# Windowed attention with value regions gathered through DRAM, one Trainium2 core: the stores of the turned values move from SyncE's queue to GpSimd's

## The reference, cut to what matters

```python
qkv = jnp.einsum('nchw,oc->nohw', xc, qkv_w) + qkv_b[None, :, None, None]
q, k, v = jnp.split(qkv, 3, axis=1)
...
a_r = q_r @ k_r
_, idx_r = jax.lax.top_k(a_r, TOPK)
...
attn = jnp.einsum('bhnqd,bhnkd->bhnqk', qs * SCALE, key_g)
attn = jax.nn.softmax(attn, axis=-1)
out = jnp.einsum('bhnqk,bhnkd->bhnqd', attn, val_g)
...
out = out + lepe
out = jnp.einsum('nchw,oc->nohw', out, out_w) + out_b[None, :, None, None]
```

## Time and profile before

| | |
|---|---|
| median of 3 runs (lowest to highest) | 1795.88 us (1792.58 to 1802.46) |
| the profiled execution, its span | 1792.81 us, 1789.8 us |
| PE, DVE, ACT, POOL busy | 91%, 86%, 77%, 59% of the span |
| granted TensorE clock | 0.996 |
| queue of SP's DMAs, of POOL's DMAs | 24.7%, 16.7% of 16 DMA engines' time |

### The profile page before, as it was taken

One profiled execution on the slowest core, in us unless ns is written; L12 is line 12 of the kernel. 1 busy time (PEld: TensorE's weight loads), 2 busy tenths in 40 slices (PEclk: granted clock), 3 DMA queues, 4 the chain that ended last, 5 costly groups with the idle time before them and its releaser, 6 DMA issues.

```text
span 1789.8 us, 73643 instructions
## 1 busy us (share of the span) xinstructions
PE 1636.2 (91%) x26568; PEld 1377.4 (77%) x26568; DVE 1530.6 (86%) x2951; ACT 1383.9 (77%) x4401; POOL 1052.2 (59%) x2548
## 2 busy tenths in 40 slices
PE   5999999999999899899999999899899999999897
PEld 4877777887778777777777788788787878777676
DVE  6589888899889889888888889899898888889895
ACT  2488778888778788788888788788787888877674
POOL 3256556566566565655565566556556666577664
PEclk9999999999999999999999999999999999999998
DMA  5233434343434343344444444434343334366555
GB/s 200 77 97 120 126 103 139 108 149 117 127 113 137 107 149 115 116 123 122 126 119 129 123 126 121 125 107 151 105 127 102 115 103 129 113 203 196 196 185 191
DMA packets 164632, 234.43 MB, mean 131 GB/s; under 512 B 19232, under 2 KB 146912, under 8 KB 164272
## 3 DMA queue, kind: packets, MB, share of 16 engines
q1 hardware_dynamic: 141408, 129.71, 24.7%
q0 software_dynamic: 22864, 100.02, 16.7%
HBM read 166.80 MB, written 62.85 MB: 128 GB/s over the span
## 4 chain that ended last, share of the span: by engine, by line
PE 61%; DVE 11%; issue 10%; ACT 9%; POOL 4%; DMA 2%; SPq 2%; POOLq 1%; ACTq 0%; DVEq 0%
PE chunk_bank L1124 20%; PE pt_bank L1240 10%; PE s_bank L1218 10%; ACT probs L744 7%; PE o_bank L1258 6%; DVE neg_max L959 5%; PE o_bank L1240 4%; PE chunk_bank L1138 3%; DVE lepe L846 2%; PE o_bank L1266 2%; POOL k_sel L502 2%; PE chunk_bank L1166 2%; PE chunk_bank L1151 1%; POOL lepe L514 1%; DMA v_sel<-v_dram 1%
## 5 line engine op out<-in xcount | busy, mean ns | idle before, releaser
L744 ACT ACTIVATE probs<-s_bank,neg_max 128x256 f32<-128x256 f32 x1568 | 734.0, 483 | 240.7 <-DVE neg_max L959 240.7
L502 POOL COPY k_sel<-k_all 128x128 f32 x1568 | 397.1, 302 | 512.4 <-PE s_bank L1218 421.9
L959 DVE TENSOR_REDUCE neg_max<-s_bank 128x2 f32<-128x512 f32 x784 | 486.8, 682 | 161.2 <-PE s_bank L1218 160.6
L846 DVE SCALAR_TENSOR_TENSOR lepe<-v_band,taps,lepe 128x448 f32<-128x448 f32 x896 | 621.3, 743 | 0.0
L1124 PE MATMUL chunk_bank<-xn,wqkv 128*128 128x224 f32 x2544 | 588.9, 357 | 29.0 <-ACT v_stage L711 13.4
L1124 PEld LDWEIGHTS chunk_bank<-xn,wqkv 128*128 128x128 f32 x2544 | 439.7, 192 | 40.9 <-issue 37.2
L754 ACT COPY probs_t<-pt_bank 128x512 f32<-128x512 f32 x611 | 364.5, 597 | 81.8 <-PE pt_bank L1240 79.3
L1240 PE MATMUL pt_bank<-ident,probs 128*128 128x128 f32 x2444 | 375.9, 276 | 22.4 <-ACT probs L744 13.3
L1240 PEld LDWEIGHTS pt_bank<-ident,probs 128*128 128x128 f32 x2444 | 281.4, 141 | 98.7 <-issue 69.4
L514 POOL TENSOR_TENSOR lepe<-o_norm,lepe 128x128 f32<-128x128 f32 x392 | 263.8, 692 | 150.7 <-DVE o_norm L982 147.3
L744 ACT ACTIVATION_READ_ACCUMULATOR probs<-s_bank,neg_max 128x1 f32 x1568 | 332.1, 212 | 0.0
(11 more groups left out here) (81 smaller groups left out, 1442.6 us busy)
## 6 DMA issues: line engine op xcount, KB each, us to landing
v_sel<-v_dram SPq DMA_DIRECT2D x1568, 64.0 KB
xn<-x_dram POOLq DMA_DIRECT2D x56, 448.0 KB, 4.9
v_dram<-v_stage SPq DMA_DIRECT2D x112, 224.0 KB
resid<-x_dram POOLq DMA_DIRECT2D x31, 448.0 KB, 4.6
out_dram<-resid POOLq DMA_DIRECT2D x31, 448.0 KB, 5.6
spill<-lepe POOLq DMA_DIRECT2D x25, 448.0 KB, 3.6
xn<-spill POOLq DMA_DIRECT2D x25, 448.0 KB, 5.5
resid<-x_dram POOLq DMA_DIRECT2D x25, 224.0 KB, 3.3
```

The source lines that it names most:

```text
L502: last = pool.tensor_copy(k_sel[:, r % K_SLOTS, :, RT * j:RT * (j + 1)], k_all[:, b % 2, :, bass.ds(reg[j] * RT, RT)])
L744: act.activation(probs[:, 2 * (j % 2) + i, :], s_bank[:, u, KEYS * at:KEYS * (at + 1)], ACT.Exp, bias=neg_max[:, h % 2, col:col + 1], accu ...
L846: ins = dve.scalar_tensor_tensor(row, v_band[:, n % BANDS, k, t // 3:t // 3 + RS, t % 3:t % 3 + W], taps[:, k, t:t + 1], row, ALU.mult, AL ...
L959: dve.tensor_reduce(neg_max[:, h % 2, 2 * j:2 * j + 2], scored, AX.X, ALU.max, negate=True).then_inc(max_done, 1)
```

## The change

Rows of image 0 are still stored by SP in the prologue. From row 7 on, `store_values` is a function of POOL's program, with the same two DMAs and two semaphores of its own, `v_kept`. POOL calls it at place 1 of the next step (`rc == 1 and rr`), so row 0's to row 5's stores stand one step later than their row; for an image's last row it calls it at place 5 of the row's own step, behind `normalize` and `load_resid`. SP's three calls are gone. The waits for stored rows, in `select_values` on SP and in `vt_out` on ACT, go through `wait_values`, which picks the semaphore by the row's number.

```diff
+        def wait_values(eng, n):
+            if n < NWIN:
+                eng.wait_ge(v_stored[n % 2], 32 * (n // 2 + 1))
+            else:
+                eng.wait_ge(v_kept[n % 2], 32 * ((n - NWIN) // 2 + 1))
...
                 if r % NREG == 0:
                     n = b * NWIN + LAST
-                    sp.wait_ge(v_stored[0], 32 * (n // 2 + 1))
-                    sp.wait_ge(v_stored[1], 32 * ((n + 1) // 2))
+                    wait_values(sp, n - 1)
+                    wait_values(sp, n)
...
                     r = s * NWIN + rc
-                    if rc == 4 and rr == LAST and is_row(kv):
-                        store_values(kv)
                     if is_region(r + 2):
                         select_values(r + 2)
-                    if rc == 0 and rr == 1 and is_row(kv - 1):
-                        store_values(kv - 1)
                     if rc == 1 and rr == LAST and is_row(kv):
                         load_index(kv // NWIN)
-                    if rc == 6 and rr not in (0, LAST) and is_row(kv):
-                        store_values(kv)
...
+            def store_values(n):
+                b, rr = divmod(n, NWIN)
+                for m in range(2):
+                    wait_taken(pool, "vt", n, m)
+                if b >= 2 and rr == 0:
+                    pool.wait_ge(attn_done, NREG * (b - 1))
+                for h in range(2):
+                    pool.dma_start(v_dram[b % 2, h:RS:2, rr * W:(rr + 1) * W, :].rearrange("q t d -> t q d"),
+                                   v_stage[PADW * h:PADW * h + W, n % 2, :, :]).then_inc(v_kept[n % 2], 16)
...
+                    if rc == 1 and rr and is_row(kv - 1):
+                        store_values(kv - 1)
+                    elif rc == 5 and rr == LAST and is_row(kv):
+                        store_values(kv)
...
                 if n >= 2:
-                    act.wait_ge(v_stored[n % 2], 32 * (n // 2))
+                    wait_values(act, n - 2)
```

More of the change, by code:

```diff
@@ L305, in attention_kernel @@
         v_stored = [sem(f"v_stored{i}") for i in range(2)]
+        v_kept = [sem(f"v_kept{i}") for i in range(2)]
         v_sel_in = [sem(f"v_sel_in{i}") for i in range(V_SLOTS)]
```

## The result

The changed kernel takes 1851.2 us (median of 4 runs, 1845.7 to 1854.0), against 1799.0 us for the kernel before, run beside it. The ratio is 1.0295, with a 95% interval from 1.0265 to 1.0326: slower by 52 us.

The account below looks back on a forecast made before the run. The prediction took PE, busy 91% of the span, as what bounds the kernel. Six image ends 27.6, image 6 7 and the clock 8.5 made 43 us, added to the profiled 1792.8: 1836 us, range 1815 to 1860.

Parts of the forecast that it names:

- the landing of the fourth load: SP's fourth value load for region 49 at an image end: estimated to land 2.5 us after issue.
- the clock: Half clock on PE behind waits of 5 us: 1.7 us at five of seven ends, 8.5 us (bounds 0 and 11.9).
- Off SP: Taking 49 rows' stores off SP's queue: worth at most 5.9 us to PE, taken as nothing.
- The 42 ordinary rows: Two issues on POOL at place 1, 1.3 us a row, covered by its waits for PE: costed at nothing.
- POOL's waits for scores: Sign in the profile after: POOL's waits for scores shorter by about 1.3 us in ordinary rows.
- Six image ends: Images 0 to 5: values land 9.05 us after `load_resid`, PE wants them at 3.8; net 4.6 us each, 27.6 us.
- The next duo's loads: Eight SP loads behind region 49's: land by about 16.1 us, PE wants them at 17.2, so the delay doesn't grow.
- What comes back: At each of six image ends, 0.65 us that PE waits for ACT shortly after is regained from the 5.25 us wait.
- Image 6: Last late end, where attention's first body is a duo: 7 us (bounds 2 and 11).
- the one with smaller waits: Rival at image ends: time given back or fast landings, 1815 us, or 1804 if half comes back too; chance 0.10.
- The one in which the store stays hidden: Rival at region 49's `attend`: values arrive in time, not slower, 1793 or 1787 us; chance 0.04.
- POOL as the bound: Rival in ordinary rows: each store issue keeps POOL 1.5 us, 47 us more, 1883 us; chance 0.06.

Follow-up runs that it names:

- experiment 1: The change, but the seven image-end stores are back on SP at their old place; 42 rows stay on POOL: 1792.2 us, 1.0007 of the kernel before.
- experiment 3: The change, but POOL issues the image-end store at place 3 instead of 5, all 49 rows on POOL: 1791.4 us, 0.9998 of the kernel before.
- Experiment 7: The change, with the x load moved from place 0 to place 3 in an image's first step: 1840.1 us, again 1840.4 against the change's 1848.1.
- experiment 6: The change plus needless matmuls ahead of the first region's `attend` of images 1 to 7: 1845.5 us with 24, 1835.2 with 12 (change beside it 1848.1).
- The kernel of place 4: The change, but POOL issues the image-end store at place 4, ahead of normalize, instead of 5: 1814.0 us, 1.0148 of the kernel before.
- the second run of the change: The change itself, unchanged, run again on a third chip beside its variants: 1848.1 us, 1.0325 of the kernel before.

## Why the prediction came out as it did

The direction and the mechanism were right, and 1851.2 us lies in the range; the predicted 1836 was 15 us short. The sizes of two terms were not right, the landing of the fourth load and the clock. Step by step:

- **Off SP: nothing.** Right. Experiments 1 and 3 equal the kernel before, and in 3 all 49 rows are off SP.
- **The 42 ordinary rows: nothing.** Right, by experiment 1. A pair of issues keeps POOL 1.38 us at the image end and 1.42 us in the row shown, against 1.3. But I had expected POOL's waits for scores to be shorter by about 1.3 us a row, some 55 us; they fell by 421.9 - 402.4 = 19.5 us. I had overlooked POOL's other pause, at `take_region`: by experiment 1 it took up 24.8 us and the waits for scores 35.0. In the change the waits at the late ends, where POOL stands for PE, add to both.
- **Six image ends, 9.05 us behind `load_resid`.** It is 11.5 us at image 0. Three terms held: the second issue at 0.69 (0.65), the landing 3.57 to 3.93 (3.6), SP's way to the fourth load 2.54 (2.3). The fourth failed: "the fourth lands 2.5 us later, an estimate between the 1.8 us [...] and the 8.48 us". It is 2.5 only where nothing follows (2.59 at image 5); five times it is 4.33 to 5.41, because POOL issues the x load of 448 KB at the same moment (305.92 and 305.93). So the six waits are 42.7 us, where 5.25 us each made 31.5. Experiment 7 shows the cause, and that it is worth about 8 us of time. Two smaller errors offset each other in the waits: the steps between the terms take some 0.6 us more, and PE comes some 0.8 us later. For the latter, POOL's next key copies do not lie under PE's wait, as I wrote, but hold up the scores ahead of it (301.83 above).
- **The next duo's loads: the delay doesn't grow.** Right: of the seven places only the last has a second wait (2.52 us).
- **What comes back, 0.65 us at each.** Right, but for one end. The first body of images 2 to 6 took 8.69, 8.62, 10.31, 8.69 and 8.62 us before, and takes 8.03 or 8.04 us behind a wait at full clock (experiment 6): 0.6 to 0.7 us come back at four ends, 2.3 us at the end of image 3.
- **Image 6: 7 us.** 5.7 us by its rows.
- **The clock: 8.5 us.** The mechanism was right, and experiment 6 shows it; the size was some 17 us: 17.5 by halving the slow work, or, at the six ends, 13.2 us by comparing the bodies with 8.03 us, where halving gives 14.0. I took the 3.5 us stretch of the earlier trace rows for the length of every one and left two ends out. All seven waits brought the clock down, and it stayed down for 3.1 to 5.8 us of work, 7.1 at image 6.

The seven places cost 63.9 us where my sum had 43; the two misjudged terms, 11 us of landings and some 8 to 9 us of clock, are most of the difference. The rest of the execution is 6.1 us shorter, which no term of mine foresaw, and so 15 us remain between the 1836 us and the profiled 1850.6. That the miss is no larger is in that part luck.

Of the rivals, the one with smaller waits fell because the waits were longer, not shorter, and little of them came back. The one in which the store stays hidden would have needed POOL to reach it earlier: experiment 3 is that case, two places up, and it gives the time of before. POOL as the bound fell with an issue of 0.69 us.

No version beat the kernel before: experiments 1 and 3 equal it within 0.3%.

Open: the 6.1 us; and why a wait of 2 to 3 us brings the clock down at one place (2.27 us in the earlier trace rows, 2.62 us in experiment 6) and not at another (2.8 us in the earlier trace rows). The kernel of place 4 adds three of each: behind waits of 3.63, 2.65 and 3.44 us the body took 9.7 us at a clock of 0.82, behind 1.71, 1.72 and 1.77 us it took 8.0 us at 1.00.

## What to carry to other kernels

A store that moves to another engine's stream must be priced where its reader is nearest, not by its average slack: 42 of 49 moves cost nothing here, seven cost everything, and two places earlier the same seven were free. A wait of TensorE costs its own length and, as behind all seven waits here, can cost half speed for what comes next; read the granted clock behind a wait of similar length before leaving it out. Estimate a short load's landing with what the other queues will issue in the same moment, not from the same load in a quiet stretch.

## What the runs showed that I had not expected

All seven waits of PE, of 4.3 to 8.1 us, were followed by work at 1.2 GHz, for up to 7.1 us of it, in a kernel whose granted clock is 0.996 over the whole of its execution before the change. The clock behind the waits is worth some 17 us, nearly a third of the loss.

At the ends of images 0 to 5 a 64 KB load of values by SP's queue lands in 2.4 to 2.6 us when no x load starts beside it, and in 4.3 to 5.4 us (3.4 to 4.4 us in the second run of the change) when one of 448 KB from POOL's queue does; the DMA engines are busy for 62% of the stretch there (306.71 to 310.40). The Trainium skill (DMA: Bandwidth & Descriptors, SWDGE vs HWDGE vs iDMA) says that inside each DMA engine the queues of the two kinds are served in turn; the trace fits that, but no run here looks into a DMA engine.
